# Layer 0 of a four-layer graph-attention kernel: clip and exponential over pairs of key blocks

## The reference

```
q, k, v = x @ Wq.T + bq, x @ Wk.T + bk, x @ Wv.T + bv      # split in 4 heads
scores  = clip(q @ k.T / sqrt(32), -10, 10)
scores  = where(adj == 0, -10, scores)                     # masked entries count as -10
attn    = softmax(scores)
out     = x + (attn @ v) @ Wo.T + bo                       # then a layer norm with gamma, beta
```

## Time and profile before

| | |
|---|---|
| median of three runs | 3339.29 us |
| the profiled execution | 3331.45 us |
| its span, first to last instruction | 3329.7 us |
| TensorE busy | 2419.7 us (73%) |
| VectorE busy | 2343.6 us (70%) |
| GpSimd busy | 1825.3 us (55%) |
| ScalarE busy | 1523.4 us (46%) |
| mean granted TensorE clock | 0.824 |

### The profile page before, as it was taken

How to read it: one execution, slowest core, us unless ns; L and a number is a source line. 1 busy time by engine, 2 the same in 40 slices (tenths; PEclk the granted TensorE clock), 3 DMA queues, 4 the chain that set the end, 5 groups by cost and what they waited for, 6 DMA issues and landing times.

```text
span 3329.7 us, 92771 instructions
## 1 busy us (share of the span) xinstructions
PE 2419.7 (73%) x33108; PEld 1668.0 (50%) x33108; DVE 2343.6 (70%) x5297; ACT 1523.4 (46%) x2211; POOL 1825.3 (55%) x1733
## 2 busy tenths in 40 slices
PE   4488888786343888888887665888555999998970
PEld 2266666564232554545454443666333666666650
DVE  3299888997665777777776545443675988888866
ACT  2355555553121443434443333444243777777760
POOL 2288777785222565555555333444232877777761
PEclk8688778887766899999998776998666988888985
DMA  6733222221454121211212542110332111111125
GB/s 218 252 92 79 72 70 70 70 69 33 127 162 153 40 56 46 52 49 50 55 46 70 144 129 75 53 46 14 124 112 64 47 47 46 43 40 47 46 44 126
DMA packets 299634, 264.33 MB, mean 79 GB/s; under 512 B 193048, under 2 KB 256792, under 8 KB 299216
## 3 DMA queue, kind: packets, MB, share of 16 engines
q1 hardware_dynamic: 294608, 241.68, 26.4%
q0 software_dynamic: 4608, 16.78, 1.4%
HBM read 162.71 MB, written 95.36 MB: 78 GB/s over the span
## 4 chain that ended last, share of the span: by engine, by line
PE 30%; issue 17%; DVE 12%; ACT 3%; POOL 3%; DMA 1%; DVEq 1%; SPq 1%; POOLq 0%; ACTq 0%
PE ps L1030 10%; PE ps L989 4%; DVE full L1328 3%; DVE full L1318 3%; PE ps L927 2%; PE ps L982 2%; POOL xg L317 2%; PE ps L987 2%; PE ps L941 2%; PE ps L889 1%; PE ps L911 1%; DVE xn L1413 1%; DVE rden L1410 1%; PE ps L973 1%; PE ps L974 1%
## 5 line engine op out<-in xcount | busy, mean ns | idle before, releaser
L317 POOL TENSOR_TENSOR xg<-xc 128x512 f16<-128x512 f32 x1536 | 1580.7, 1053 | 836.1 <-ACT xc L800 703.1
L1030 PE MATMUL ps<-vs,xc 128*128 128x33 bf16 (+1 forms) x13824 | 850.4, 189 | 143.0 <-DVE work L1376 89.7
L1030 PEld LDWEIGHTS ps<-vs,xc 128*128 128x128 bf16 x13824 | 679.2, 101 | 471.2 <-issue 295.2
L1030 PE MATMUL ps<-vs,xg 128*128 128x33 bf16 (+1 forms) x9216 | 778.5, 187 | 0.0
L1030 PEld LDWEIGHTS ps<-vs,xg 128*128 128x128 f16 x9216 | 596.7, 99 | 3.1 <-issue 3.1
L800 ACT ACTIVATE xc<-ps 128x512 f32<-128x512 f32 x512 | 305.7, 597 | 436.7 <-PE ps L974 436.5
L800 ACT ACTIVATE xc<-cv,lift 128x512 f32<-128x512 f32 x512 | 351.2, 718 | 295.1 <-DVE cv L1351 293.8
L1328 DVE CUSTOM_DVE_ANT_0 full<-ps,mask_n 128x512 bf16<-128x512 f32 x512 | 353.0, 690 | 169.2 <-PE ps L941 61.6
L1318 DVE CUSTOM_DVE_ANT_0 full<-ps,mask_n 128x1024 bf16<-128x1024 f32 x320 | 390.4, 1220 | 105.4 <-PE ps L927 76.0
L989 PE MATMUL ps<-qs,sel 128*128 128x512 f32 x640 | 415.5, 651 | 0.0
L1351 DVE SCALAR_TENSOR_TENSOR cv<-ps,mask_t 128x512 f32<-128x512 f32 x512 | 336.3, 684 | 60.4 <-PE ps L970 37.9
(11 more groups left out here) (138 smaller groups left out, 3739.7 us busy)
## 6 DMA issues: line engine op xcount, KB each, us to landing
qs<-q_d SPq DMA_DIRECT2D x224, 128.0 KB
ks<-k_d SPq DMA_DIRECT2D x224, 128.0 KB
part<-row_d SPq DMA_DIRECT2D x40, 512.0 KB
v_d<-vbuf SPq DMA_DIRECT2D x24, 792.0 KB, 4.2
vs<-v_d SPq DMA_DIRECT2D x96, 198.0 KB
q_d<-part SPq DMA_DIRECT2D x32, 512.0 KB
k_d<-part SPq DMA_DIRECT2D x32, 512.0 KB
ctx_d<-xn SPq DMA_DIRECT2D x96, 128.0 KB, 1.7
```

Of the source, the lines that this page charges most:

```text
L317: eng.tensor_tensor(plo[:, r, :], prob[:, r, :], phi[:, r, :], ALU.subtract).then_inc(low_done(layer, u, s)[0], 1)
L1030: mm = pe.matmul(acc, half[:, r, it * P:(it + 1) * P], vs[:, n, at:at + width], start=opens and h == 0 and v == 0, stop=h == 1 and v == 1, ...
```

## The change

In layer 0 the clip and the exponential take two tiles (two neighbouring key blocks, two PSUM banks) in one instruction of 1024 elements a partition. `settle_two(s)` and `exp_two(s)` run at even s; `arg` becomes a ring of eight slots, and cv grows from two to four rows, of which xT and neg now have the last two; xg is gone. s_p counts one for each pair in layer 0, so `settled_before` and all that is counted from it changes. TensorE waits for the clip once for each pair.

The lag of `weigh` in layer 0 goes from six tiles to ten, so that `blocks_done` takes e = s - 11, and the rings of `prob` and `plo` from 8 to 16 slots (in all layers). `prob` moves to the memory of part, `plo` to that of xc, and the row buffer `si8` of layers 2 and 3 from part to ks. The products of a pair go to one of four banks, 4 to 7, in place of two, and wait for the pair four before. `blk` is laid out with each key block's 128 values in sequence: the multiply writes in sequence, and the reduction reads its eight values with a step of 128 floats.

```diff
-DEEP = 8
-LAGS = (6, 6, 6, 6)
+DEEP = 16
+LAGS = (10, 6, 6, 6)
...
-HLEFT = (4, 4, 6, 3)
+HLEFT = (7, 4, 6, 3)
...
-        blk = work[:, :, :].rearrange("p t f -> p (t f)").rearrange("p (t d j) -> p j t d", d=32, j=BLOCKS)
+        blk = work[:, :, :].rearrange("p j (t d) -> p j t d", d=32)
...
+                    def exp_two(s):
+                        T, r, a = tile_value(s), s % DEEP, s % (2 * RING)
+                        act.wait_ge(s_p, p_at(s))
+
+                        act.wait_ge(s_av, T - DEEP + 2)
+                        act.activation(prob[:, r:r + 2, :], arg[:, a:a + 2, :], ACT.Exp,
+                                       scale=2.0 * CLIP, bias=lift[:, 0:1]).then_inc(s_exp, 2)
...
-                        exps(s)
+                        if layer:
+                            exps(s)
+                        elif s % 2 == 0:
+                            exp_two(s)
...
-                                if not (first and s < RING):
-                                    pe.wait_ge(s_p, T - CREDIT - RING + 1)
+                                if s % 2 == 0 and not (first and s < RING):
+                                    pe.wait_ge(s_p, settled_before(layer, u, s - RING) + 1)
...
-                                pe.wait_ge(s_chfree, CREDIT + u * (TILES // 2 * UNROLL) + s // 2 - 1)
+                                pe.wait_ge(s_chfree, CREDIT + u * (TILES // 2 * UNROLL) + s // 2 - 3)
...
-                                acc = ps[:, 6 + s // 2 % 2, (s % 2 * IB + it) * 33:(s % 2 * IB + it + 1) * 33]
+                                acc = ps[:, 4 + s // 2 % 4, (s % 2 * IB + it) * 33:(s % 2 * IB + it + 1) * 33]
...
+                    def settle_two(s):
+
+                        T, r, a = tile_value(s), s % RING, s % (2 * RING)
+                        c, j = s // BLOCKS % 2, s % BLOCKS
+                        dve.wait_ge(s_score, T - CREDIT + 2)
+                        dve.wait_ge(s_exp, T - 2 * RING + 2)
+                        dve.scalar_tensor_tensor(arg[:, a:a + 2, :], ps[:, r:r + 2, :], -0.5,
+                                                 mask_t[:, j:j + 2, c * HALF:(c + 1) * HALF], ALU.max, ALU.min
+                                                 ).then_inc(s_p, 1)
...
-                        if s < total and layer != 1 and s % RING not in RELU_AT[layer]:
+                        if layer == 0 and s < total and s % 2 == 0:
+                            settle_two(s)
+                        if layer > 1 and s < total and s % RING not in RELU_AT[layer]:
                             settle(s)
```

More of the change, by code:

```diff
@@ L135, in build @@
         xn = sb("xn", [P, 2, BLOCKS, F])
-        cv = sb("cv", [P, 2, NODES])
+        cv = sb("cv", [P, 4, NODES])
         cT, vf = cv[:, 0, :], cv[:, 1, :].rearrange("p (t f) -> p t f", f=F)
-        xg = sb("xg", [P, 2, NODES])
-        xT, neg = xg[:, 0, :], xg[:, 1, :].rearrange("p (t f) -> p t f", f=F)
+        xT, neg = cv[:, 2, :], cv[:, 3, :].rearrange("p (t f) -> p t f", f=F)
         bns = sb("bns", [P, BLOCKS, 6])
@@ L162, in build @@
         colx = sb("colx", [P, UNROLL, 3, BLOCKS])
-        prob = xc[:, :, :, :].rearrange("p a t f -> p (a t f)").rearrange("p (r n) -> p r n", n=HALF)
+        flat = part[:, :, :, :, :].rearrange("p g a b n -> p (g a b n)").bitcast(F32)
+        prob = flat.rearrange("p (r n) -> p r n", n=HALF)
         arg = cv[:, :, :].rearrange("p a n -> p (a n)").rearrange("p (r n) -> p r n", n=HALF)
[L168 to L172, removed]
+        phi = flat.bitcast(BF16).rearrange("p (r n w) -> p r n w", n=HALF, w=2)[:, :, :, 1]
+        plo = xc[:, :, :, :].rearrange("p a t f -> p (a t f)").bitcast(F16).rearrange("p (r n) -> p r n", n=HALF)
+        si8 = ks[:, :, :].bitcast(F32)
         junk = full[:, 1, :].bitcast(BF16)[:, 0:NODES]
@@ L322, in settled_before, with arg_at @@
             if layer == 0:
[L323 to L327, removed]
+                return u * (TILES // 2 * UNROLL) + s // 2
+            return TILES // 2 * UNITS[0] + TILES // 2 * (UNIT0[layer] - UNIT0[2]) + u * (TILES // 2 * UNROLL) + s // 2
+        def arg_at(s):
+            return s // 2 % RING
         def stored_before(layer, u, n):
@@ L793, in exps @@
                             n, j = s // TILES, s % BLOCKS
-                            src, more = arg[:, arg_at(layer, s), :], dict(bias=cols[:, n, 1, j:j + 1])
-                            if layer == 0:
-                                more = dict(scale=2.0 * CLIP, bias=lift[:, 0:1])
+                            src, more = arg[:, arg_at(s), :], dict(bias=cols[:, n, 1, j:j + 1])
                         act.wait_ge(s_av, T - DEEP + 1)
@@ L979, in scores @@
                             if s % RING in RELU_AT[layer]:
-                                pe.wait_ge(s_relu, settled_before(layer, u, s) - TILES * UNITS[0] + 1)
+                                pe.wait_ge(s_relu, settled_before(layer, u, s) - TILES // 2 * UNITS[0] + 1)
                                 pe.matmul(bank, ident_b[:, :], mask_t[:, j, cut], start=False, stop=False,
@@ L1341, in tile_value @@
                         return CREDIT + TILES * UNIT0[layer] + u * (TILES * UNROLL) + s
+                    def settle_two(s):
[6 more added lines that the diff above has]
+                                                 ).then_inc(s_p, 1)
                     def settle(s):
                         T, r = tile_value(s), s % RING
[L1347 to L1361, removed]
+                        n, c, j = s // TILES, s // BLOCKS % 2, s % BLOCKS
+                        dve.wait_ge(s_score, T - CREDIT + 1)
+                        dve.wait_ge(s_exp, T - 2 * RING + 1)
+                        dve.scalar_tensor_tensor(arg[:, arg_at(s), :], si8[:, n, c * HALF:(c + 1) * HALF],
+                                                 colx[:, n, 0, j:j + 1], ps[:, s % RING, :], ALU.max, ALU.add
+                                                 ).then_inc(s_p, 1)
                     def out_free(n):
@@ L1476, in _ @@
             heads(0)
-            dve.wait_ge(s_p, TILES * UNITS[0])
+            dve.wait_ge(s_p, TILES // 2 * UNITS[0])
             dve.tensor_scalar(mask_t[:, :, :], mask_t[:, :, :], 0.5, BIG, ALU.subtract, ALU.mult
```

2 lines of the change are left out of this document (1 added, 1 removed).

## The result

| | before | after |
|---|---|---|
| median | 3339.36 us (4 runs) | 3306.26 us (3301.97 to 3311.36, 4 runs) |
| ratio | | 0.9898, 95% interval 0.9866 to 0.993 |
| profiled execution, span | 3331.45, 3329.7 us | 3308.95, 3307.3 us |
| layer 0, first score matmul to the mask conversion behind it | 637.9 us | 605.4 us |
| layer 1, first row-maximum matmul to the last score matmul | 729.1 us | 735.3 us |

33 us faster by the medians. The two profiled executions are 22 us apart: layer 0 is 32.5 us shorter, and the other stages together 10 us longer, of which layer 1 has 6.

What follows compares the result with a forecast made beforehand. VectorE was taken to bound layer 0, with losses to a TensorE falling to half clock. Layer 0: 566 + 16 + 8 + 13 = 603 us, 35 less than 638; total forecast 3299 us, range 3266 to 3334.

Steps and rivals of the forecast that it cites:

- VectorE's work: Layer 0: VectorE's half of a unit falls from 9.20 to 8.84 us, 566 us in all, 23 less.
- the multiply's occupation: Layer 0's multiply, writing in sequence, takes 0.20 us less a pair, 0.80 a half, 51 us.
- Waits away from the borders: Layer 0, VectorE waiting for TensorE at low clock after its stop: 0.25 us a half, 16 us, against 18 now.
- the lead of four steps: Four product banks let TensorE run four steps ahead of VectorE in layer 0, instead of two.
- Borders: Between layer 0's eight loop bodies VectorE loses 1.2 us a border, 8 us, against 20 before.
- Filling and draining: Start and end of layer 0: 11 us, and 2 more for longer lag and last reduction.
- The edits at nothing: Sixteen slots, moved buffers and SP queue cause no new waits; layers 1 to 3 stay within 2 us.
- TensorE's stop after the reduction: In layer 0 TensorE stands still some 2.2 us behind the longer reduction, and its clock falls again.
- GpSimd came level with VectorE: Rival: strided reads cost less and GpSimd becomes layer 0's bound; 73 us less, 3262; chance 0.10.
- A longer stay at the low level: Rival: TensorE stays at low clock two pairs or more after each reduction; 18 us less, 3318; chance 0.17.
- The multiply kept its 643 ns: Rival: layer 0's multiply stays slow because of its three-dimensional pattern; 2 us more, 3338; chance 0.11.
- The low level throughout: Rival: TensorE bounds all of layer 0 at low clock; 660 us, 22 more, total 3356; chance 0.07.

Runs made afterwards that it cites:

- e9: Kernel before with only four banks of products and the wait for the pair four before: 3307.36 us, ratio 0.9922, layer 0 610.0 us.
- e8: Kernel before with only the memory moves and 16 slots instead of 8: 3335.99 us, ratio 1.0002, layer 1 733.4 us.
- e12: e3 with 8 slots instead of 16 in layers 1 to 3: 3253.55 us, ratio to before 0.9766, layer 1 732.0 us.
- e2: Changed kernel with the old block-sum layout, the multiply walking a pair's two key blocks innermost: 3260.68 us, ratio to before 0.9757.
- e3: Changed kernel with a pair's 256 block sums in sequence, its two blocks side by side: 3252.54 us, ratio to before 0.9756.
- e4: Changed kernel with two banks of products and the wait for the pair two before: 3618.16 us, ratio to before 1.0835.
- e1: Changed kernel with the old layout of the block sums: 3295.87 us, ratio to before 0.9881, layer 0 592.6 us.
- e7: Kernel before with only the new layout of the block sums: 3350.61 us, ratio 1.0050, layer 0 652.0 us.
- e5: Changed kernel with a lag of six tiles in layer 0 instead of ten: 3318.06 us, ratio to before 0.9935.
- e6: Changed kernel with the clip as two instructions of 512 elements, each after its own scores: 3310.98 us, ratio to before 0.9942.

## Why the prediction was right, and where it was not

The forecast was 3299, the result 3306; layer 0 was put at 603 us and took 605. The mechanism is the one forecast: VectorE bounds layer 0, less its waits on a TensorE at the low level. But the sum came out so close by luck: VectorE's work was put 14 us too low, and the waits and ends together 12 us too high.

- **VectorE's work** (forecast 566 us, measured 64 x 9.07 = 580). The step that failed is the multiply's occupation. I took 0.20 us, nearly the whole 0.22 between the records, off the distance to the next clip. The strided multiply's record overlapped the next clip by some 0.17 us (0.64 against 0.47), the sequential one's by 0.08 (0.42 against 0.34), so the saving was 0.12 to 0.13 in three of a half's four multiplies and 0.23 in the last. I had used this very rule for the clips, where it held, and not here. The reduction was put at 1901 and took 1992, 6 us in all.
- **Waits away from the borders** (forecast 16 us, measured 19.0 - 9.6 = 9.4, of which 2.2 are at the first five clips; before 37.9 - 13.1 = 24.8). I named the lead of four steps and then gave it almost nothing, 2 us. e9 shows that it is worth 28 us of layer 0 by itself. This is the main cause of the gain, and the forecast had it as a side line.
- **Borders** (forecast 8 us, against 20 before; measured 9.6, against 13.1). There are five, not seven; all that the change does to them won 3.5 us, not 12.
- **Filling and draining** (forecast 13, 6 left over, before 11). This is what the other terms leave of the stretch, not a time that was measured. Not all of it is at the ends: an instruction that waits loses the overlap with the one before it, 0.07 to 0.17 us, 74 times before and 33 times after, by my estimate 5 and 3 us.
- The edits at nothing: no DMA and no wait of the other layers for a slot showed up, but layer 1, which was to stay within 2 us, took 6 more, and why stays open (e8, e12). TensorE's stop after the reduction was put at some 2.2 us; 2.2 is the longest of them, the middle one 1.5. The exponential took 1151 ns, not 1056, without cost: ScalarE is busy 295 of 605 us.
- **Rivals.** GpSimd came level with VectorE only in e2 and e3. A longer stay at the low level did not come: the clock rose to 0.86. The multiply kept its 643 ns in no kernel in which it writes in sequence. The low level throughout came in e4, where it costs far more than the 22 us I gave it, because a ring of waits comes with it.

Put together: of the 32.5 us that layer 0 lost, 8 are VectorE's work, 15 its waits away from the borders, 4 the borders, 5 what is left over. By edits, on layer 0: four banks -28 (e9 against before), the layout +13 (after against e1) or +14 (e7), lag -12 (e5 against after), pairs -6 (e6 against after). That these add up to -33 proves little, since each was taken at one place, and e4 shows how strongly banks and pairs hang together.

## What to carry to other kernels

Before shortening a bound engine's instructions, ask how many steps its supplier may run ahead, and which buffer sets that: one more pair of banks was worth more than all edits to the instructions in this change (28 us of the 32.5). The wider instruction has a price of its own, as it waits for the last of its inputs. Price an instruction by the distance between starts, not by its record, for the new form too. When data is written in one order and read in another, look for the order in which both sides touch two neighbouring values; it cost nothing here and gave 47 us against the changed kernel, 42 against the old layout (e1).

## What the runs showed that I had not expected

- A strided SBUF read of 128 sums of eight took 1992 ns here and 1901 in the row of node(3), in sequence 1220; a write with a step of 32 bytes took 643 ns, and 426 with two neighbouring floats a step.
- Waiting for two tiles at once with two banks of products closed a ring that took 3.41 us a pair against 1.71, with the granted clock at 0.50 in the mean of 915 us.
- The exponential of 1024 elements took 1151 ns, an exponential of the same size in node(), which reads no bias column, 1056.
